# Turning rows of q and of the score weights into columns: TensorE transposes and VectorE sums in place of folding matmuls

## What is computed

```python
q = cond @ Wq.T + bq                    # one row per batch, 16 heads of 32
k = x @ Wk.T + bk
v = x @ Wv.T + bv
q = q / sqrt(32)
scores = einsum('bhqd,bhkd->bhqk', q, k)[:, :, 0, :]
attn = clip(scores, 0.0, 1.0)
context = attn[..., None] * v
return x + context @ Wo.T + bo
```

## Time and profile before

| | us |
|---|---|
| median of 3 executions | 186.25 |
| lowest and highest | 186.05 and 186.3 |
| the profiled execution, own time | 186.12 |
| its span, first to last instruction | 184.3 |
| PE busy | 180.6 |
| VectorE busy | 169.8 |
| ScalarE busy | 115.7 |
| granted TensorE clock, mean | 0.998 |

### The profile page before, as it was taken

The page is one execution under the profiler, slowest core; times in us unless marked ns, Lnnn a source line. Parts: engine busy times, 40 slices in busy tenths (PEclk is TensorE's granted clock), DMA queues, the critical chain, the costliest instruction groups (busy, mean ns, idle before and its releaser), DMA issues.

```text
span 184.3 us, 2383 instructions
## 1 busy us (share of the span) xinstructions
PE 180.6 (98%) x803; PEld 147.7 (80%) x803; DVE 169.8 (92%) x186; ACT 115.7 (63%) x158; POOL 14.3 (8%) x20
## 2 busy tenths in 40 slices
PE   8999999999999999999999999999999999999993
PEld 2788888888878888888888888888888888888883
DVE  1999997998699999999999999999999999989963
ACT  3789873796587754765667764783486854766200
POOL 8000000000000020121000010111000001111000
PEclk9999999999999999999999999999999999999999
DMA  6999910027701017289568617399920207489786
GB/s 216 345 392 429 401 63 2 0 59 233 283 13 44 21 36 117 114 131 230 94 244 282 238 39 114 121 147 312 274 119 0 57 0 115 131 127 295 132 343 228
DMA packets 9355, 30.13 MB, mean 163 GB/s; under 512 B 1152, under 2 KB 1536, under 8 KB 9216
## 3 DMA queue, kind: packets, MB, share of 16 engines
q1 hardware_dynamic: 7616, 23.70, 35.6%
q0 software_dynamic: 1728, 6.29, 20.6%
HBM read 19.50 MB, written 8.39 MB: 151 GB/s over the span
## 4 chain that ended last, share of the span: by engine, by line
PE 98%; DVE 0%; issue 0%
PE bank_y L354 9%; PE bank_y L358 9%; PE bank_y L356 9%; PE bank_x L354 8%; PE bank_x L358 8%; PE bank_x L356 8%; PE bank_z L354 6%; PE bank_z L358 6%; PE bank_z L356 6%; PE bank_x L429 4%; PE score_bank L415 4%; PE score_bank L414 4%; PE bank_z L429 3%; PE bank_z L474 2%; PE bank_x L447 2%; PE bank_y L447 1%
## 5 line engine op out<-in xcount | busy, mean ns | idle before, releaser
L858 DVE TENSOR_TENSOR form_lo<-work,form_hi 128x1024 fp32r<-128x1024 f32 (+1 forms) x38 | 40.3, 1081 | 2.9 <-ACT form_hi L579 2.6
L579 ACT CAST form_hi<-work 128x1024 fp32r<-128x1024 f32 x28 | 29.1, 1051 | 20.7 <-PE score_bank L415 6.9
L614 ACT ACTIVATE work<-bank_y,const 128x512 f32<-128x512 f32 x30 | 19.7, 686 | 9.2 <-PE bank_y L358 9.2
L841 POOL DMA_DIRECT2D work<-x_t x12 | 10.5, 875 | 154.8 <-DVE work L891 148.0
L354 PE MATMUL bank_x<-form_hi,wo_hi 128*128 128x512 f32 x52 | 20.3, 391 | 0.0
L358 PE MATMUL bank_x<-form_hi,wo_lo 128*128 128x512 f32 x52 | 20.2, 389 | 0.0
L356 PE MATMUL bank_x<-form_lo,wo_hi 128*128 128x512 f32 x52 | 20.2, 389 | 0.0
L614 ACT ACTIVATE work<-bank_x,const 128x512 f32<-128x512 f32 x24 | 15.9, 685 | 6.4 <-PE bank_x L358 5.8
L880 DVE SCALAR_TENSOR_TENSOR work<-relu,work 128x1024 f32<-128x1024 f32 x16 | 19.4, 1220 | 0.3 <-ACT relu L643 0.3
L354 PE MATMUL bank_y<-form_hi,wv_hi 128*128 128x512 f32 x48 | 18.7, 389 | 0.0
L356 PE MATMUL bank_y<-form_lo,wv_hi 128*128 128x512 f32 x48 | 18.7, 389 | 0.0
(11 more groups left out here) (150 smaller groups left out, 389.8 us busy)
## 6 DMA issues: line engine op xcount, KB each, us to landing
x_raw<-x_t SPq DMA_DIRECT2D x16, 512.0 KB, 6.3
out_t<-work SPq DMA_DIRECT2D x14, 512.0 KB, 3.6
work<-x_t POOLq DMA_DIRECT2D x12, 512.0 KB, 5.9
score_others<-score_rows SPq DMA_DIRECT2D x16, 128.0 KB, 2.3
work<-first_t SPq DMA_DIRECT2D x2, 512.0 KB, 3.7
work<-wq_t SPq DMA_DIRECT2D x2, 512.0 KB, 8.0
work<-wk_t SPq DMA_DIRECT2D x2, 512.0 KB, 11.0
work<-wo_t SPq DMA_DIRECT2D x1, 1024.0 KB, 13.4
```

Source lines behind the costliest of these rows:

```text
L579: nc.scalar.copy(flat(form_hi, kind), raw(kind, phase)).then_inc(hi_ready[kind], 1)
L614: nc.scalar.activation(result_set(phase)[:, q, j * ROWS:(j + 1) * ROWS], of[:, j, :], ACT.Identity, bias=bias[:, tile:tile + 1], scale=sca ...
L841: pool.dma_start(output_set(s)[:, q, :], x_t[s, q], accum_op=ALU.add).then_inc(residual_added[q], 16)
L858: return nc.vector.tensor_tensor(to, of, hi.bitcast(F32), ALU.subtract)
```

## The change

The four folding matmuls for q and the four for the score weights become TensorE transposes (`pe.transpose`: the rows as one operand, an identity as the other). They take only the rows in use: 4 in place of 128 for q, 64 in place of 128 for the score weights. The outputs hold both parts side by side, so they have twice the columns (4 and 64 per block), in the same bank as before. The sum of the parts moves to VectorE: one addition more in `scale_q` (128 x 8) and one more in `fill_a` (128 x 128), each with a wait on the instruction before it. The waits on `q_sum_ready` and `a_full_ready` count one more. The two folding tables in `const` make room for one identity of 64, and `const` grows from 202 to 232 columns. Nothing else is moved.

```diff
-C_FOLD = C_HEAD + HEADS
-C_PAIR = C_FOLD + BATCH * HEADS
-C_COND = C_PAIR + BATCH
+C_ONE = C_HEAD + HEADS
+C_COND = C_ONE + 2 * BATCH * HEADS
...
-        q_psum = score_bank[1][:, 0:MT * BATCH].rearrange("p (m b) -> p m b", m=MT)
-        a_psum = score_bank[1][:, P:P + KT * BATCH * HEADS].rearrange("p (k n) -> p k n", k=KT)
+        q_psum = score_bank[1][:, 0:2 * MT * BATCH].rearrange("p (m s b) -> p m s b", m=MT, s=2)
+        a_psum = score_bank[1][:, P:3 * P].rearrange("p (k s n) -> p k s n", k=KT, s=2)
...
             for m in range(MT):
-                mm = pe.matmul(q_psum[:, m, :], q_rows[:, m * P:(m + 1) * P], const[:, C_PAIR:C_PAIR + BATCH],
-                               start=True, stop=True)
+                n = 2 * BATCH
+                mm = pe.transpose(q_psum[:, m, :, :], q_rows[0:n, m * P:(m + 1) * P], const[0:n, C_ONE:C_ONE + n])
             mm.then_inc(q_done, 1)
...
             for k in range(KT):
-                mm = pe.matmul(a_psum[:, k, :], a_rows[:, k * P:(k + 1) * P], const[:, C_FOLD:C_FOLD + BATCH * HEADS],
-                               start=True, stop=True)
+                n = 2 * BATCH * HEADS
+                mm = pe.transpose(a_psum[:, k, :, :], a_rows[0:n, k * P:(k + 1) * P], const[0:n, C_ONE:C_ONE + n])
             mm.then_inc(a_done, 1)
...
-                nc.vector.tensor_tensor(q_sum[:, :, :], q_psum, bq.unsqueeze(2).to_broadcast([P, MT, BATCH]),
+                nc.vector.tensor_tensor(q_sum[:, :, :], q_psum[:, :, 0, :], bq.unsqueeze(2).to_broadcast([P, MT, BATCH]),
                                         ALU.add).then_inc(q_sum_ready, 1)
                 dve.wait_ge(q_sum_ready, 1)
+                nc.vector.tensor_tensor(q_sum[:, :, :], q_sum[:, :, :], q_psum[:, :, 1, :], ALU.add).then_inc(q_sum_ready, 1)
+                dve.wait_ge(q_sum_ready, 2)
...
-                nc.vector.tensor_copy(a_full[:, 0:KT, :], a_psum).then_inc(a_full_ready, 1)
+                nc.vector.tensor_copy(a_full[:, 0:KT, :], a_psum[:, :, 0, :]).then_inc(a_full_ready, 1)
                 dve.wait_ge(a_full_ready, 1)
+                nc.vector.tensor_tensor(a_full[:, 0:KT, :], a_full[:, 0:KT, :], a_psum[:, :, 1, :], ALU.add).then_inc(a_full_ready, 1)
+                dve.wait_ge(a_full_ready, 2)
...
-    for first in (0, BATCH * HEADS):
-        const[first:first + BATCH * HEADS, C_FOLD:C_FOLD + BATCH * HEADS] = np.eye(BATCH * HEADS)
-    for first in (0, BATCH):
-        const[first:first + BATCH, C_PAIR:C_PAIR + BATCH] = np.eye(BATCH)
+    const[0:2 * BATCH * HEADS, C_ONE:C_COND] = np.eye(2 * BATCH * HEADS)
```

More of the change, by code:

```diff
@@ L1070, in scale_bk @@
             def scale_bk():
-                dve.wait_ge(q_sum_ready, 1)
+                dve.wait_ge(q_sum_ready, 2)
                 nc.vector.scalar_tensor_tensor(
@@ L1077, in fill_a @@
                 dve.wait_ge(a_done, 1)
-                nc.vector.tensor_copy(a_full[:, 0:KT, :], a_psum).then_inc(a_full_ready, 1)
+                nc.vector.tensor_copy(a_full[:, 0:KT, :], a_psum[:, :, 0, :]).then_inc(a_full_ready, 1)
                 dve.wait_ge(a_full_ready, 1)
+                nc.vector.tensor_tensor(a_full[:, 0:KT, :], a_full[:, 0:KT, :], a_psum[:, :, 1, :], ALU.add).then_inc(a_full_ready, 1)
+                dve.wait_ge(a_full_ready, 2)
                 nc.vector.tensor_tensor(a_full[:, KT:KT + 2, :], a_full[:, 2:4, :], a_full[:, 0:2, :], ALU.subtract).then_inc(a_full_ready, 1)
             def split_a(b):
-                dve.wait_ge(a_full_ready, 2)
+                dve.wait_ge(a_full_ready, 3)
                 dve.wait_ge(zeros_ready, 4)
```

## The result

| us | before | after |
|---|---|---|
| median of 16 executions each | 186.10 | 185.67 |
| lowest and highest | 185.64 and 186.39 | 184.92 and 186.09 |
| the profiled execution, own time | 186.12 | 185.97 |
| its span | 184.3 | 184.2 |
| wv lands behind its issue | 5.5 | 6.3 |

The ratio of the times is 0.9975, with a 95% interval of 0.9965 to 0.9985: 0.43 us less in the medians, where 0.69 were summed up from the rows. The change makes the kernel faster, by just over what can be told from nothing.

A forecast was written before the change was run, and what follows sets the result against it. PE was taken as the bound, working without a stop after its opening; 0.24 us at q plus 0.45 at the score weights made 0.69 off, 185.43 to 185.56, stated as 185.5 us, range 185.2 to 186.3.

The forecast's parts named there:

- Four records in place of eight: On PE at L490 and L506: each transpose runs as one record, saving 4 records per group.
- The price of a transpose: On PE in both groups: one record at a pitch of 0.1125 us, saving 0.45 us per group.
- faster still: Rival: a transpose takes a quarter of the fp32 pair, 0.056 us; 0.92 us saved, 185.2 us; chance 0.12.
- The rival built on it: Transposes on PE don't overlap, each waiting for the last: 0.39 us more, 186.5 to 186.6 us; chance 0.14.
- The q term: At PE's weight load for rows with Wk: of 0.45 us saved, VectorE's later result costs 0.21, 0.24 kept.
- The score-weight term: At the score-weight group: 0.45 us kept, the 0.33 us addition fitting into 0.58 us of room.
- idle time forecast before `fill_a`: On VectorE before it fills the score weights: idle for some 0.3 us in place of 1.16.
- Nothing for the table: Load of const: 30 more columns, 15 KB, cost nothing.
- B11 as the next in line: PE's load for B11 after VectorE's remainder: 0.5 us of room, the first place to show unabsorbed VectorE lateness.
- From the scores on all rows earlier by the same amount: From scores(0, 0), starting near 32.4 in place of 33.07, every PE row is earlier by the same amount.
- The hand-over: From the end of VectorE's result to PE's waiting weight load: 0.17 us, read elsewhere in the trace.

The follow-up runs named there:

- fourfold_turn: Changed kernel with scale_q ahead of wo_sum(0) on VectorE, each score-weight transpose issued four times (16 in all): 185.97 us, ratio to before 0.9994.
- q_only: Kernel before with only q turned by transposes, with its added addition; score weights still folded by matmuls: 186.36 us, ratio to before 1.001.
- no_adds: Changed kernel without its two added VectorE additions: 185.48 us, ratio to before 0.9964.
- a_only: Kernel before with only the score weights turned by transposes, with their added addition; q still folded by matmuls: 185.77 us, ratio to before 0.9982.
- early_scale: Changed kernel with scale_q moved ahead of wo_sum(0) on VectorE: 185.14 us, ratio to before 0.9953.
- const_only: Kernel before with the table of constants widened from 202 to 232 columns, the rest unchanged: 186.17 us, ratio to before 1.000.
- earlier_scale: Changed kernel with scale_q moved ahead of both wk_part(3) and wo_sum(0) on VectorE: 185.21 us, ratio to before 0.9954.
- early_before: Kernel before, folding matmuls kept, with scale_q moved ahead of wo_sum(0) on VectorE: 185.57 us, ratio to before 0.9981.

## Why the prediction was right, and where it was off

**Direction and range: right.** Faster, with the measured 185.67 within 185.2 to 186.3 and 0.17 above the forecast.

**Four records in place of eight: right.** Both groups show it.

**The price of a transpose: right in the sum, wrong in its make-up.** The prediction took one record at 0.1125 us and saved 0.45 per group. A transpose costs 0.065, near the quarter of the pair (0.056) of the "faster still" rival. But entering the group and leaving it has a toll: 20.28 is where the last of the four matmuls ahead starts, and the transposes begin at 20.60, 0.32 later in place of 0.23; behind the fourth the product comes 0.13 after it. The savings were 0.39 and 0.41. The errors cancelled, so that the sum came out is luck. By the Trainium skill (TensorE: Matmul & The Clock Gate, Terms) the mode is four times faster for FP32, which the pitch roughly agrees with (0.225 for a pair, 0.065: 3.5 times), though the transposes here also load fewer rows, 4 or 64, and no run has one of 128; the page doesn't give the toll. Its 275 ns (Part 4) would as a pitch have made the twelve transposes of `fourfold_turn` cost 3.3 us, and they cost 0.80: the durations here are 0.20 to 0.27, so it is a duration. The rival built on it is out.

**The q term, 0.24 us kept: the step that failed.** It read VectorE's room at L453 off one execution (ready 23.93, load 24.43) and took that room as a property of the kernel. In most profiles it isn't there: VectorE's chain starts where wv lands, up to 1.0 us later than in that one, while PE had been slower than usual in its opening (11.01 in place of 10.4 to 10.6). With the usual landing the q part gives nothing or costs its addition (`q_only`, 1.0010). The prediction had the mechanism, the wait of L453 for L858, and even the sign of what is lost; it mis-sized it, 0.21 us foreseen against all of the saving in a usual execution. Set to about 0 the sum is 0.4, near the 0.43 that came out. That the forecast was only 0.17 off is luck in part: in a kernel whose PE isn't held, both savings reach the end in full (`no_adds` against before, 0.8 us from the opening to B11, though without the additions). Nor do the halves add up: `q_only` lost 0.2 and `a_only` gained 0.33 on one chip, which makes 0.1, where the whole gave 0.43 and 0.5 on two others. With about 0.3 us of uncertainty on the halves alone this is at the edge of the noise; whether wv lands earlier on those chips, no run shows.

**The score-weight term, 0.45 us kept: right.** 0.41 on PE, 0.33 (0.11 to 0.54) at the end in `a_only`, the addition at 0.32 for 0.33 foreseen, no wait before the scores. The cover was thinner than said on one side: of the 0.3 us of idle time forecast before `fill_a` 0.1 was there, PE's folding still setting the start. With the earlier `scale_q` it is VectorE that sets it: `early_scale` has no idle time there.

**Nothing for the table: right.** `const_only`, ratio 1.000.

**B11 as the next in line: right.** It showed as soon as L453 was freed (`early_scale`, `earlier_scale`).

**From the scores on all rows earlier by the same amount: right.** From the first matmul of `scores(0, 0)` to PE's last one it takes 148.01 us before and after. But the scores start at 32.96, not near 32.4, and the load at L453 at 24.83, not near 24.3: the hold at L453 again.

**The hand-over, 0.17 us: too long.** At L453 it takes 24.83 - 24.78 = 0.05 in the profile after and the same in `const_only`; at B11 about 0.2; the 0.17 of the earlier trace rows isn't a constant. With 0.05 the q term would have come out 0.12 larger, so this didn't cause the miss.

**What stays open:** what makes wv land early or late, and what makes PE's opening slow or fast. It is not the table and not the change: wv lands after 5.5 us with 202 columns (before) and with 232 (`no_adds`), after 6.1 us and more with either, and slow openings come with either too. Open, too, is by how much the halves miss the whole.

## What to carry to other kernels

A wait list that is empty tells that a wait didn't happen in this execution, not that there is room; where the room hangs on a transfer of the opening, look at a second profile before a saving is counted against it. When an engine's list is shortened ahead of a join, compute what the other side of the join does, and look there first for something that may go behind the result that is waited for: here two lines swapped on VectorE were worth 0.35 us on the kernel before (`early_before`), nearly as much as the 0.43 of the whole change on PE. And once the swap is made, VectorE's work ahead of the next join sets the end, so that a further swap brings nothing.

## Of the hardware, not expected

- An fp32 transpose on TensorE with 64 or 4 rows of 128 columns runs as one record at a pitch of 0.065 us, where a folding fp32 matmul runs as two at 0.10 to 0.1125. The rows are the weight loads and the transposes of the profile after, ns at least, in the middle and at most:

```profile
L490 PEld LDWEIGHTS score_bank<-const,relu x4: 133/136/138, 20.6 to 20.8; 4*128 4x128 f32 x4
L490 PE MATMUL score_bank<-const,relu x4: 197/198/220, 20.6 to 20.8; 4*128 4x4 f32 x4
...
L506 PE MATMUL score_bank<-const,relu x4: 222/223/272, 29.7 to 29.9; 64*128 64x64 f32 x4
```

- Going from matmuls to transposes and back costs about 0.1 us each way, once per group: 0.21 us from L502 to the first transpose against 0.13 to the first folding matmul (29.71 - 29.50, 29.32 - 29.19), and 0.13 to 0.15 from the last transpose to the product.
- The same load at the same place in the same queue lands after 5.5 us in some executions and after 6.1 to 6.5 in others, and moves VectorE's whole first phase with it; in this kernel the end moves only where PE waits for VectorE.
- PE's first matmuls of 512 columns start some 0.43 us apart in place of 0.23 until 6.1 to 6.7 us in four of fourteen profiles and until 5.1 to 5.6 us in ten; the first four leave the opening 0.3 to 0.9 us later. The listed granted clock is 1.00 in before and in after alike.
